# Copy order in the first chunk, W V ahead of chunk 16's exponents, and no keys for the last chunk of each sequence

## The reference

```python
Q, K, V = x @ Wq.T, x @ Wk.T, x @ Wv.T            # heads of 64, 64, 16
g = -exp(A_log) * softplus(x @ Wdt.T + dt_bias)
Lam = softplus(Lp * (x @ Wdl.T))                  # 12 levels per head
cg = cumsum(g, axis=1)
decay = exp(where(tri, cg[t] - cg[s], -1e30))
lam_ts = Lam[t, level(t, s)]                      # level from t XOR s
W = (Q @ K.T) / 8 * decay * lam_ts                # per head, causal
o = (W @ V) @ Wout.T + x                          # then layer norm, residual, layer norm
```

## Time and profile before

| | us |
|---|---|
| median of 3 runs | 687.79 (687.26 to 689.74) |
| profiled execution | 687.91 |
| its span | 686.1 |
| TensorE busy | 665.7 (97%) |
| DVE busy | 474.0 (69%) |
| GpSimd busy | 348.1 (51%) |
| ScalarE (ACT) busy | 339.3 (49%) |

### The profile page before, as it was taken

The page is one execution under the profiler, slowest core; times in us unless marked ns, Lnnn a source line. Parts: engine busy times, 40 slices in busy tenths (PEclk is TensorE's granted clock), DMA queues, the critical chain, the costliest instruction groups (busy, mean ns, idle before and its releaser), DMA issues.

```text
span 686.1 us, 22147 instructions
## 1 busy us (share of the span) xinstructions
PE 665.7 (97%) x9194; PEld 602.8 (88%) x9194; DVE 474.0 (69%) x1072; ACT 339.3 (49%) x759; POOL 348.1 (51%) x471
## 2 busy tenths in 40 slices
PE   9999999999999999999999999999978999999994
PEld 7889999999999999899999999999967788888894
DVE  3765786869786868658696868688896445454546
ACT  5565444454555454544545555545433434555555
POOL 2715563647556565556474555665455215343434
PEclk9999999999999999999999999999997899999998
DMA  9213030302222130203031221303032000000002
GB/s 299 61 29 91 8 97 8 94 24 76 50 51 55 46 83 18 67 6 95 22 79 47 54 52 48 88 13 84 2 99 62 1 1 1 32 32 32 32 32 92
DMA packets 53588, 37.09 MB, mean 54 GB/s; under 512 B 5360, under 2 KB 52080, under 8 KB 53488
## 3 DMA queue, kind: packets, MB, share of 16 engines
q1 hardware_dynamic: 53488, 35.67, 19.1%
HBM read 30.41 MB, written 5.24 MB: 52 GB/s over the span
## 4 chain that ended last, share of the span: by engine, by line
PE 90%; DVE 3%; ACT 2%; SPq 1%; DMA 1%; issue 1%; POOL 1%; DVEq 0%; ACTq 0%; POOLq 0%
PE bank L383 66%; PE bank L386 6%; PE bank L407 5%; PE bank L474 5%; PE bank L439 5%; PE bank L503 4%; SPq L330 1%; DMA xt<-in_wffn 1%; DVE t L985 1%; ACT t L751 1%; ACT E L751 0%; DVE t L988 0%; DVE st L1285 0%; DVE hh L985 0%; DMA scr<-cT 0%
## 5 line engine op out<-in xcount | busy, mean ns | idle before, releaser
L383 PE MATMUL bank<-xH,wH 128*128 128x256 f32 x480 | 144.4, 301 | 1.2 <-ACT KT L751 0.9
L383 PE MATMUL bank<-xL,wH 128*128 128x256 f32 x480 | 135.0, 281 | 0.0
L383 PE MATMUL bank<-xH,wL 128*128 128x256 f32 x480 | 134.4, 280 | 0.0
L985 DVE TENSOR_TENSOR W<-bank,E 128x512 f32<-128x512 f32 x128 | 82.2, 685 | 31.3 <-PE bank L383 31.3
L383 PEld LDWEIGHTS bank<-xH,wH 128*128 128x128 f32 x480 | 90.4, 188 | 7.6 <-issue 7.0
L383 PEld LDWEIGHTS bank<-xL,wH 128*128 128x128 f32 x480 | 90.6, 189 | 0.4
L383 PEld LDWEIGHTS bank<-xH,wL 128*128 128x128 f32 x480 | 90.5, 188 | 0.0
L751 ACT ACTIVATE E<-bank 128x512 f32<-128x512 f32 x128 | 66.1, 604 | 47.7 <-PE bank L407 47.7
L751 ACT ACTIVATE QT<-bank 128x512 f32<-128x512 f32 x64 | 38.2, 596 | 101.3 <-PE bank L383 101.3
L383 PE MATMUL bank<-QT,KT 64*128 64x128 f32 x1024 | 65.8, 278 | 1.6 <-ACT E L751 1.6
L383 PEld LDWEIGHTS bank<-QT,KT 64*128 64x128 f32 x1024 | 59.7, 188 | 6.0 <-ACT E L751 1.8
(11 more groups left out here) (151 smaller groups left out, 1678.0 us busy)
## 6 DMA issues: line engine op xcount, KB each, us to landing
cB<-scr SPq DMA_DIRECT2D x240, 64.0 KB, 2.9
xt<-in_xT SPq DMA_DIRECT2D x16, 256.0 KB, 2.9
xs<-in_x SPq DMA_DIRECT2D x16, 256.0 KB, 3.2
out<-xs SPq DMA_DIRECT2D x16, 256.0 KB, 2.1
xt<-in_wffn SPq DMA_DIRECT2D x8, 256.0 KB, 3.1
QT<-in_wqk SPq DMA_DIRECT2D x4, 256.0 KB, 5.8
KT<-in_wqk SPq DMA_DIRECT2D x4, 256.0 KB, 7.1
scr<-cT SPq DMA_DIRECT2D x16, 64.0 KB, 1.9
```

The costliest lines, as they stand in the source:

```text
L383: return e.matmul(o, a, b, start=start, stop=stop)
L985: return e.tensor_tensor(o, a, b, op)
```

## The change

Six edits. On TensorE, for chunk 16 alone, `weigh(15, .)` comes ahead of `exponents(16)`. `keys(15)` and `keys(31)` are left out, on TensorE and on ACT, and the banks and counts that went with them are counted anew (each takes two uses, so the others keep their banks). `decays(1)` comes behind `project(1, 3)`; later supergroups keep the old order. On ACT the copy of projection (1,1) comes ahead of the two copies of `keys(0)`.

```diff
 def misc_jobs(s):
-        if s % 4 == 0:
+        if s % 4 == 0 and cc < CB - 1:
             out += [("keys", ci, 0), ("keys", ci, 1)]
 # TensorE
             for s in STEPS:
                 ci, n = s // 4, s % 4
-                if 0 <= ci < NC and n == 0:
+
+                late = 0 <= ci < NC and n == 0 and ci - 1 not in STATE and ci
+                if 0 <= ci < NC and n == 0 and not late:
                     exponents(ci)
                 if (c1 := chunk_at(s, 4)) is not None:
                     weigh(c1, 0)
                     weigh(c1, 1)
+                if late:
+                    exponents(ci)
                 if 0 <= ci < NC:
-                    if n == 0:
+                    if n == 0 and ci in STATE:
                         keys(ci)
...
                 for sg, j in token_jobs(s):
-                    if j == 3:
+                    if j == 3 and sg > 1:
                         decays(sg)
                 for sg, j in project_jobs(s):
                     project(sg, j)
+                for sg, j in token_jobs(s):
+                    if j == 3 and sg == 1:
+                        decays(sg)
 # ACT
             def keys(ci):
-                    e.wait_ge(p_kt, 2 * ci + n + 1)
+                    e.wait_ge(p_kt, 2 * STATE[ci] + n + 1)
...
-                if 0 <= s < NG and s % 4 == 0:
+                if 0 < s < NG and s % 4 == 0 and s // 4 in STATE:
                     keys(s // 4)
                 for sg, j in project_jobs(s):
                     project(sg, j)
+                if s == 0:
+                    keys(0)
                 for sg, j in token_jobs(s):
```

## The result

The changed kernel takes 690.31 us (median of 12 executions, 689.87 to 691.55), the kernel before 687.51 (12 executions, 686.11 to 689.74). The ratio is 1.0040, 95% interval 1.0031 to 1.0049, so the change costs 2.1 to 3.4 us. Against the kernel before beside it the change costs 2.8 us where +0.1 was forecast, and the range that the terms of the sum gave, 687.2 to 688.6, does not hold the result: only the wider range does, which was drawn to take in the rival with the clock.

A forecast was written before the change was run, and what follows sets the result against it. TensorE, busy for 97% of the span, was taken to bound the kernel. Terms of +0.9 (first chunk), -1.0, +0.2 and 0 summed to +0.1 us, giving 687.9 us, with a stated range of 686.4 to 690.9.

The forecast's parts named there:

- the wider range: Whole kernel: 686.4 to 690.9 us, holding the forecast, most of the clock cases and the partly faster ones.
- the rival with the clock: TensorE's clock falls behind the 2.9 or 2.8 us idle: 689.4 us for one fall, 690.8 for both; chance 0.30.
- Part 1: First chunk: ACT copies projection (1,1) first; (1,2) starts 0.9 us earlier, but (1,3) still waits until 41.03; worth 0.
- Part 2: First chunk: supergroup 1's decays behind projection (1,3) put their whole time on the path, +0.90 us, between 0.6 and 1.15.
- Part 3: Chunk 15: eight transposes leave an unbroken TensorE stretch and DVE moves along; -1.0 us, between -0.85 and -1.1.
- Part 4: Border of chunks 15 and 16: W V waits for DVE's output sum of chunk 14; +0.22 us, between +0.1 and +0.4.
- Part 5: Chunk 31: without keys TensorE idles 2.8 us and still goes on at 518.51; worth 0, between -0.15 and +0.1.
- The sum: Whole kernel: +0.9 - 1.0 + 0.2 + 0 = +0.1 us, hence 687.9; by the terms' ends 687.2 to 688.6.
- the slower rival: The clock falls behind TensorE's longer idle times at the start or chunk 31: 689.4 or 690.8 us; chance 0.30.

The follow-up runs named there:

- decays_back: The changed kernel with the decays of supergroup 1 back ahead of projection (1,3) on TensorE; 688.79 us, ratio 1.0021.
- fill_start: The changed kernel with six unread fp32 products of 256 columns between projections (1,2) and (1,3); 688.54 us, ratio 1.0011.
- fill_end: The changed kernel with 8 and 6 unread fp32 products of 256 columns in TensorE's two waits at chunk 31; 688.08 us, ratio 1.0015.
- start_alone: The kernel before with only the first chunk's two edits, of decays(1) and of ACT's keys(0); 689.03 us, ratio 1.0027.
- no_keys31: The kernel before without the keys of chunk 31, on TensorE and ACT; 688.63 us, ratio 1.0020.

## Why the prediction was right, and where it was not

Four of the five parts came as placed, to 0.2 us. The sum didn't, and the time lies in the stated range only because the range took in a rival held for less likely.

**Part 1, copies turned, worth 0.** Right: (1,2) follows the scores, the wait ahead of (1,3) is 2.91 us (2.9 forecast), and decays_back, which keeps this edit, has the first chunk of before to 0.01 us.

**Part 2, decays on the path, +0.90.** Right: 0.83 to 0.90 (fill_start, fill_end, start_alone, each less 14.17).

**Part 3, keys of chunk 15, -1.0.** The mechanism is right, the term was too large. It measured -0.81, just outside the bounds; the nearer row was the start-to-start 0.84 of the earlier trace rows, not the middle with the busy time, in which neighbours overlap.

**Part 4, border, +0.22.** Right: 0.18 to 0.20, with DVE's output sum as releaser.

**Part 5, keys of chunk 31, 0.** Right for the start of the scores (1.66 us behind the weight copy, 1.65 before), wrong as the end of the matter. The transposes were work in a wait. Without them the kernel before is 1.15 us slower by the median (no_keys31), though its one profile hardly shows it in the pieces; three useless products in that wait bring it back.

**The sum.** The forecast of +0.1 assumed that the clock stays where it was. That is the step that failed, and the slower rival is what happened: the clock fell behind the 2.9 us wait, at 1.6 us in place of my 1.46, and stayed low through the one of 2.45. I gave it 0.30 with the argument that neither wait reaches 3.8 us. Of the four profiled executions with that wait at the start and no products in it two show the fall, so it deserved at least the weight of the forecast. The rival's 690.8 for falls behind both waits comes within 0.5 us of the 690.31, but not by its own working: the second fall shows no 1.5 us in the pieces (chunk 31 is 0.30 shorter than before), so part of that nearness is luck.

**What stays open.** By the pieces the changed kernel loses 1.6 us (2.0 less the 0.39 of loading); by the medians 2.8, at least 2.1. Part of the gap is that the profiled executions lie on opposite sides of their medians (687.91 against 687.51, 689.91 against 690.31). Another part may be that the profile of the kernel before has the long piece to the gate, 17.97, where others with the same mean clock have 16.30. The clock is the candidate for the rest. The mean clock of the 12 executions is 0.978 to 0.983, against 0.983 to 0.986 for the 35 of before; as (1 - clock) x span x 2 that is 26.6 and 20.9 us at the low level. fill_end brings it to 15.8 and gains 2.2 us for 10.8 us less of it, about 0.2 us for each, since much of it lies under waits (in the changed kernel the clock is low from 513 on, but the scores of chunk 31 start with E in any case); at the start the price is higher, 1.6 us. No trace shows the unprofiled executions, so which stretches they lose is argued, not shown.

## What to carry to other kernels

When an engine waits for a copy, look up what is queued ahead of that copy on its own engine: here one activation, waiting for a DVE chain, decided the first chunk, and moving the copy past it took 0.55 us off that chunk in the traces, where the reordering on TensorE took off nothing. Work that lies in a wait costs nothing, so moving it out costs its full time, and taking it away buys nothing. And a wait that gets longer on TensorE has a second price, the clock, so two schedules with the same critical instructions can differ by 1.6 us.

## What I had not expected of the hardware

Useless products made the kernel faster: with six fp32 products of 256 columns in a wait of the first chunk the median fell from 690.31 to 688.54, and three at chunk 31 brought no_keys31 from 688.63 to 687.28. They aren't safe, though: the kernel before with fourteen of them at chunk 31 is 0.8 us slower. Two traces of the same start (2.91 and 2.92 us of wait) differ by 1.56 us, because the clock fell in one and not in the other. The clock also falls without a wait just ahead of it: at 526 in the kernel before, in a gapless row of products of two columns, when TensorE had been at work since 518.51. And the loading ahead of the first chunk varies by 1.6 us between executions of code that is the same there.
